# Building one batch's factor stack on two queues, ahead of that batch's input, and moving its use forward on TensorE

## The reference

```python
z1 = jnp.einsum('bfi,bir->bfr', x, v[:, 0]) / inch      # inch = 512; v and u are the same factor f
z = jnp.einsum('bfr,bor->bfo', z1, u[:, 0]) / r         # r = 16
y = jnp.einsum('bfi,oi->bfo', x, W) + fc_bias + z + b   # b = cond
return x + gelu(y)                                      # exact gelu
```

## Time and profile before

| | us |
|---|---|
| median of three runs | 380.36 |
| the profiled execution's own time | 380.21 |
| its span, first to last instruction | 378.3 |
| PE busy | 369.9 (98%) |
| PEld busy | 360.3 (95%) |
| DVE busy | 297.8 (79%) |
| ACT busy | 204.2 (54%) |
| SP's DMA queue (q1), share of 16 DMA engines | 73.1% |

### The profile page before, as it was taken

How to read it: one execution, slowest core, us unless ns; L and a number is a source line. 1 busy time by engine, 2 the same in 40 slices (tenths; PEclk the granted TensorE clock), 3 DMA queues, 4 the chain that set the end, 5 groups by cost and what they waited for, 6 DMA issues and landing times.

```text
span 378.3 us, 7905 instructions
## 1 busy us (share of the span) xinstructions
PE 369.9 (98%) x3111; PEld 360.3 (95%) x3111; DVE 297.8 (79%) x184; ACT 204.2 (54%) x210; POOL 0.7 (0%) x5
## 2 busy tenths in 40 slices
PE   8889999999999999999999999999999999999995
PEld 3679999999999999999999999999999999999984
DVE  6599788887789877788877888878788887788832
ACT  5376455664455664545665445675445665445532
POOL 0000000000000000000000000000000000000000
PEclk9999999999999999999999999999999999999999
DMA  7879989868686768787678786768777678783223
GB/s 238 212 208 342 291 235 280 252 223 264 215 259 216 213 225 260 215 263 225 202 218 264 221 257 214 213 229 253 224 251 227 204 230 250 227 258 127 113 111 113
DMA packets 27725, 85.50 MB, mean 226 GB/s; under 512 B 6784, under 2 KB 7168, under 8 KB 23744
## 3 DMA queue, kind: packets, MB, share of 16 engines
q1 hardware_dynamic: 27568, 85.19, 73.1%
q10 hardware_dynamic: 144, 0.13, 0.1%
HBM read 35.75 MB, written 33.55 MB: 183 GB/s over the span
## 4 chain that ended last, share of the span: by engine, by line
PE 97%; issue 1%; ACT 1%; DVE 0%; POOLq 0%; ACTq 0%
PE y L473 86%; PE update L559 4%; PE y L457 2%; PE y L465 2%; PE y L461 2%; PE update L539 1%; ACT result L306 0%; PE y L566 0%; DVE result L402 0%; POOLq L58 0%; DVE full_w L351 0%; ACT w_high L285 0%; ACTq L265 0%; POOLq L633 0%
## 5 line engine op out<-in xcount | busy, mean ns | idle before, releaser
L473 PE MATMUL y<-x_high,w_high 64*128 64x512 f32 x960 | 215.7, 386 | 1.3 <-ACT result L306 1.3
L473 PE MATMUL y<-x_low,w_high 64*128 64x512 f32 x960 | 215.6, 386 | 0.0
L306 ACT ACTIVATE result<-y,bias 128x512 f32<-128x512 f32 x129 | 81.4, 682 | 158.7 <-PE y L473 150.9
L473 PE MATMUL y<-x_high,w_low 64*128 64x512 f32 x960 | 135.5, 386 | 0.0
L402 DVE TENSOR_TENSOR result<-result,x_in 128x1024 f32<-128x1024 f32 (+1 forms) x66 | 78.4, 1189 | 54.8 <-ACT result L306 54.8
L473 PEld LDWEIGHTS y<-x_high,w_high 64*128 64x128 f32 x960 | 118.6, 184 | 1.7 <-issue 1.7
L473 PEld LDWEIGHTS y<-x_low,w_high 64*128 64x128 f32 x960 | 118.6, 184 | 0.0
L473 PEld LDWEIGHTS y<-x_high,w_low 64*128 64x128 f32 x960 | 111.3, 184 | 0.0
L351 DVE SCALAR_TENSOR_TENSOR full_w<-update,base_w 128x2048 f32<-128x2048 f32 (+2 forms) x36 | 73.9, 2054 | 20.3 <-PE update L559 18.5
L347 DVE TENSOR_TENSOR w_low<-full_w,w_high 128x2048 fp32r<-128x2048 f32 (+1 forms) x35 | 73.6, 2102 | 0.3
L347 DVE TENSOR_TENSOR x_low<-x_in,x_high 128x2048 fp32r<-128x2048 f32 (+1 forms) x35 | 73.5, 2101 | 0.0
(11 more groups left out here) (19 smaller groups left out, 23.1 us busy)
## 6 DMA issues: line engine op xcount, KB each, us to landing
out_t<-result SPq DMA_DIRECT2D x63, 512.0 KB, 3.4
x_in<-x_t SPq DMA_DIRECT2D x31, 1024.0 KB, 6.3
f_stack<-f_parts SPq DMA_DIRECT2D x183, 64.0 KB, 4.0
f_stack<-f_parts SPq DMA_DIRECT2D x122, 32.0 KB, 4.0
x_in<-x_first SPq DMA_DIRECT2D x4, 256.0 KB, 4.1
base_w<-w_t SPq DMA_DIRECT2D x4, 256.0 KB, 4.3
f_parts<-factors SPq DMA_DIRECT2D x1, 768.0 KB, 8.2
f_parts<-factors SPq DMA_DIRECT2D x2, 128.0 KB, 5.1
```

What stands on the lines that cost most here:

```text
L306: nc.scalar.activation(result[j % SLOTS][:, m, cols], y[m][:, cols], ACT.Gelu, bias=bias[:, bass.ds(b * CHUNKS + m, 1)]).then_inc(gelu_rea ...
L473: return nc.tensor.matmul(y[m][:, :], w[rows, c, m * P:(m + 1) * P], x[rows, c, :], start=first, stop=last)
```

## The change

Four things change. (1) The function `stack_factors` takes the issuing engine and a range of its five transfers. (2) For batch 1, SP issues the first three transfers (`ACT_PARTS = 3`) and ScalarE the last two, on its own queue, between `x_high` and `w_high` of chunk 1; ScalarE waits for `f_low_ready` first. (3) On SP the load of batch 1's x moves from ahead of `cond` to behind these three transfers. (4) On TensorE `rank_update(0, 1)` moves from the middle of the third piece of batch 0 to its head. Besides, `factors` lies in DRAM group by group (8 blocks of 64 rows of 512) instead of row by row with the groups inside. The matmuls, the transfers and their bytes are the same.

```diff
+    ACT_PARTS = 3
+        def stack_factors(engine, t, j, first=0, last=PART_DMAS):
+            parts = f_parts[j * RANK:(j + 1) * RANK, bass.ds(t, 1), :, :].rearrange("r a h i -> r (a h) i")
+            ...
+            blocks = ((0, slice(0, 2), high.to_broadcast([RANK, 2, FEATURES])), (1, slice(0, 2), parts[:, 0:2, :]),
+                      (2, slice(0, 1), low), (2, slice(1, 2), high),
+                      (3, slice(0, 2), low.to_broadcast([RANK, 2, FEATURES])))
+            for copy in range(1 if in_whole(t, j) else TILES):
+                row = copy * TILE
+                for g, sides, pair in blocks[first:last]:
+                    engine.dma_start(f_stack[slot][row + g * RANK:row + (g + 1) * RANK, sides, :].bitcast(fp32),
+                                     pair).then_inc(stacked[slot], 16)
...
-            sp.dma_start(f_first[P - RANK:P, :], factors[0:RANK, 0, :]).then_inc(f_first_loaded, 16)
+            sp.dma_start(f_first[P - RANK:P, :], factors[0, 0:RANK, :]).then_inc(f_first_loaded, 16)
...
-            sp.dma_start(f_parts[:, 0, 2, :], factors[:, 0, :]).then_inc(f_loaded[0], 16)
+            sp.dma_start(f_parts[:, 0, 2, :], factors[0]).then_inc(f_loaded[0], 16)
...
-            load_x(sp, 0, 1)
             sp.dma_start(cond_sb[:, :, :], cond).then_inc(bias_loaded, 16)
             sp.dma_start(fc_sb[:, :], fc_bias).then_inc(bias_loaded, 16)
             sp.wait_ge(f_low_ready, 1)
-            stack_factors(0, 1)
-            sp.dma_start(f_parts[:, 1, 2, :], factors[:, 1, :]).then_inc(f_loaded[1], 16)
-            stack_factors(0, 2)
+            stack_factors(sp, 0, 1, last=ACT_PARTS)
+            load_x(sp, 0, 1)
+            sp.dma_start(f_parts[:, 1, 2, :], factors[1]).then_inc(f_loaded[1], 16)
+            stack_factors(sp, 0, 2)
             load_x(sp, 0, 2)
...
-                    sp.dma_start(f_parts[:, 2:GROUPS, 2, :], factors[:, 2:GROUPS, :]).then_inc(f_loaded[2], 16)
+                    sp.dma_start(f_parts[:, 2:GROUPS, 2, :], factors[2:GROUPS].rearrange("g r i -> r g i")).then_inc(f_loaded[2], 16)
...
+                if b == 0 and c == 1:
+                    act.wait_ge(f_low_ready, 1)
+                    stack_factors(act, 0, 1, first=ACT_PARTS)
                 act.wait_ge(full_w_ready, CHUNKS * b + c + 1)
...
+                if n == HALF + 1:
+                    rank_update(0, 1)
                 pe.wait_ge(x_high_ready, n)
...
-                if n == HALF + 1:
-                    rank_update(0, 1)
                 pe.wait_ge(w_low_ready, n)
```

More of the change, by code:

```diff
@@ L39, in cond_residual_kernel @@
     GROUPS = BATCHES // UNROLL
-    RANK = factors.shape[0] // UNROLL
+    RANK = factors.shape[1] // UNROLL
     UPDATE_SCALE = 1.0 / (FEATURES * RANK)
@@ L177, in store @@
                              result[j % SLOTS][:, chunks, cols]).then_inc(stored[j % SLOTS], 16)
+        def stack_factors(engine, t, j, first=0, last=PART_DMAS):
+            parts = f_parts[j * RANK:(j + 1) * RANK, bass.ds(t, 1), :, :].rearrange("r a h i -> r (a h) i")
+            slot = j % SLOTS
+            high, low = parts[:, 0:1, :], parts[:, 1:2, :]
+            blocks = ((0, slice(0, 2), high.to_broadcast([RANK, 2, FEATURES])), (1, slice(0, 2), parts[:, 0:2, :]),
[6 more added lines that the diff above has]
+                                     pair).then_inc(stacked[slot], 16)
         block = ctx.enter_context(nc.Block())
@@ L225, in step @@
                     sp.wait_ge(update_ready, made(b + 1))
-                    stack_factors(t3, j3)
+                    stack_factors(sp, t3, j3)
                 if is_first(t, j):
-                    sp.dma_start(f_parts[:, 2:GROUPS, 2, :], factors[:, 2:GROUPS, :]).then_inc(f_loaded[2], 16)
+                    sp.dma_start(f_parts[:, 2:GROUPS, 2, :], factors[2:GROUPS].rearrange("g r i -> r g i")).then_inc(f_loaded[2], 16)
                     load_x(sp, 0, 3)
@@ L627 @@
     factors = np.asarray(fside_Bx1x1024x16_0).reshape(batches // UNROLL, UNROLL, P, chunks, rank)
-    factors = np.ascontiguousarray(factors.transpose(1, 4, 0, 3, 2).reshape(UNROLL * rank, batches // UNROLL, features))
+    factors = np.ascontiguousarray(factors.transpose(0, 1, 4, 3, 2).reshape(batches // UNROLL, UNROLL * rank, features))
     x_first = np.ascontiguousarray(x[0].T.reshape(P, chunks, rows).transpose(1, 0, 2))
```

## The result

The changed kernel is slower: median 381.85 us over 22 runs against 380.04 over 22 of the kernel before, ratio 1.0047, 95% interval 1.0029 to 1.0064. I had forecast 377.6 and "faster". The profiled execution took 382.76, with a span of 381.0. Three runs beside the experiments that took 680 us and more are left out of every median and ratio here.

The account below looks back on a forecast made before the run. TensorE bound the kernel, with two waits before 23.36 us hanging on batch 1's late stack. With batch 1's x as the new bound, its products start at 20.7: 380.21 - 2.65 = 377.56, stated 377.6, range 376.8 to 379.2.

Parts of the forecast that it names:

- The update on TensorE: Batch 1's update at the head of batch 0's third piece: due at 13.10 without waiting, TensorE 1.6 us earlier.
- batch 1's stack: Three transfers on SP, no longer behind x: 3.5 us to land, at 12.3, in time for 13.10.
- ScalarE's issues: ScalarE's two stack issues cost 0.75 to 1.4 us; the shift of later chunks was put at nothing.
- VectorE: full_w of batch 1 starts at 14.3 to 14.6, ends at 16.9; alone it would allow batch 1's products at 20.1.
- Batch 1's x as the new bound: Its load, issued at 9.5 behind three stack transfers, takes 6.2 us, lands at 15.7 and sets batch 1's start.
- The restart: Batch 1's products on TensorE start at 20.7 (15.7 + 1.8 + 3.2) instead of 23.36, 2.65 us earlier.
- the sum: The whole start-up gain reaches the end: 380.21 - 2.65 = 377.56 us, stated as 377.6; 66% for this forecast.
- What is late next: Checks after batch 1's start: its w_low, batch 2's stack and x, batch 3's x all arrive in time; no loss.
- The last line of the prediction: Sign of being wrong: TensorE stops later on w_low or a stack, which the sum does not hold; no size given.
- SP's later loads 1.0 us earlier: With two issues fewer on SP, batch 2's x is issued about 1.0 earlier, at 17.1 instead of 18.12.
- Rival C: Batch 1's x load takes 9.7 us or more, landing 19.2; products start at 24.2, 0.84 us lost, 381.1; 8%.
- Rival A: SP's and ScalarE's queues take turns issuing: x lands at 17.1, products start at 22.1, 1.3 us won, 379.0; 12%.

Follow-up runs that it names:

- e6: e4 with all five transfers of batch 1's stack on SP again, none on ScalarE: 378.63 us, ratio 0.9962 to the kernel before.
- e11: The changed kernel run again, unaltered: 381.35 us, ratio 1.0041 to the kernel before.
- e4: The changed kernel with batch 4's x load issued behind batch 4's stack instead of ahead: 378.27 us, ratio 0.9961 to the kernel before.
- e9: The changed kernel with both moves, those of e1 and e4: 378.31 us, ratio 0.996 to the kernel before.
- e1: The changed kernel with the 768 KB load of later factors issued about 25 us later: 378.82 us, ratio 0.9968 to the kernel before.
- e2: The kernel before with only the 768 KB load of later factors issued later: 379.79 us, ratio 0.9994.
- e10: The kernel before with only batch 4's x load issued behind batch 4's stack: 380.12 us, ratio 1.0004.
- e3: The changed kernel with the old layout of the factors in DRAM: 380.06 us, ratio 1.001 to the kernel before.
- e5: The kernel before with a second 768 KB load, into a buffer nothing reads, behind the first: 384.36 us, ratio 1.011.
- e8: e4 with batch 1's x load ahead of cond and of batch 1's stack again: 383.00 us, ratio 1.0078 to the kernel before.

## Why the prediction was wrong

- **The update on TensorE, batch 1's stack, ScalarE's issues, VectorE:** right. The update starts with no wait. The five transfers take 2.9 to 3.6 us, where I took 3.5. ScalarE's two issues take 1.39, my upper end, and full_w of chunk 3 (12.95 + 0.68 = 13.63) is still ahead of 14.00.
- **Batch 1's x as the new bound:** right. Its load takes 5.6 us (I took 6.2), x_high then starts with idle time that ends by the DMA, and w_high follows at once; the rows that answer to the earlier trace rows:

```profile
8.25 1.39 ACTq L191 DMA_DIRECT2D f_stack<-f_parts  x2
...
16.23 1.92 ACT L266 ACTIVATE x_high<-x_in 128x2048 fp32r<-128x2048 f32 x1 [1.93 <-DMA x_in<-x_t]
18.05 1.90 ACT L272 ACTIVATE w_high<-full_w 128x2048 fp32r<-128x2048 f32 x1
```

- **The restart** follows the line of x to 0.02 us: it comes 5.0 us behind x_high's start (1.8 + 3.2 in the sum) in every trace with x behind the stack but that of e6 (5.2). But with two issues on ScalarE x went out at 9.9 to 10.9 instead of 9.5 and landed at 16.0 to 17.1 instead of 15.7. So the restart, 20.7 by the sum, was 21.24 here, 21.42 in e11, 21.0 in e4 and e9 and 22.08 in e1: 1.3 to 2.35 us won instead of 2.65. Even without the later wait the medians (e4 378.27, e9 378.31) stay 0.7 above 377.6.
- **"What is late next" is the step that failed.** The sum books the whole gain to the end on the condition "as long as nothing later comes late", and puts later waits at nothing. I followed batch 2's stack and batch 3's x and stopped there. Batch 4's stack, behind nearly 4 MB in a full queue, had 1.1 us of slack in the kernel before, and a gain of 2 us ran into it: 1.91 us of wait (1.20 in e11). It shows in the trace of before: one issue and one landing, compared with the update that uses them. The last line of the prediction ("a later stop of TensorE on w_low or a stack, which this sum does not hold") named the hole without looking into it.
- **SP's later loads 1.0 us earlier** failed too: 18.64 for batch 2's x, not 17.1. f_low_ready came 0.8 later in this execution, SP's three issues took 0.77 each (0.68 for each of the five before), and the ten of batch 2 took 6.78 instead of 6.51. It was no accident of this execution: 18.55 in e11, where f_low_ready was in time, and 18.2 to 19.2 in all traces of this start. Batch 2's stack, forecast to land at 18.8, landed at 20.2 here and in e11, where TensorE waited 0.27 us for it (0.53 in e1), hidden behind x. And with SP's list behind, the floor itself rose from 44.6 to 45.1 (e11) and 45.6.
- **The clock** was in no term and in no rival. Without it the answer would have been "no change"; with it, slower.
- **Rival C** had the right side and the wrong mechanism: x came in time. Rival A did not come: the five issues on two queues took 2.30 us from first to last here and 2.74 in e11, not the 3.41 of one queue. But that is more than the 2.04 (three times 0.68) of the forecast, so part of the saving was lost.

## What to carry to other kernels

Before a start-up gain is booked to the end, follow each prefetched buffer to its first use and write down landing and use; the smallest slack, here 1.1 us three batches later, caps the gain. Where the DMA queue is full, a faster consumer gains nothing until the transfer it will wait for is moved ahead of those that it does not need yet; the same reorder without the faster consumer gained nothing here either (e2, e10), so the two must be tried together. A new wait of TensorE in mid-run can cost more than its length: in the traces of the changed kernel and of e3 the batch after the wait took another 1.7 us, at the lower clock.

## What the runs showed of the hardware that I had not expected

- In the profiled executions, TensorE's granted clock stayed at 1.00 after waits of 1.20 us (e11), 1.56 us (the kernel before, at 15.07) and 1.65 us (e5), and fell to 0.50 after waits of 1.91 (changed kernel), 2.26 (e3) and 3.90 us (e8). In the changed kernel it stayed low for about 3.4 us. Of runs of one kernel, some had it and some not.
- SP's first stack issues took 0.68 us each with all five on SP (3.41 for five) and 0.69 (2.07 for three, e8), 0.77 (2.30, changed kernel) to 0.93 (2.78, e3) with two on ScalarE, which took 0.70 each, against 0.37 for ScalarE's store. That ScalarE's issues slow SP's is not shown: ten issues of SP with nothing beside them took 6.50 (e5) to 7.79 us (e3), 0.65 to 0.78 each.
